# Opening joined with the first attention; gathered stages that take y's sums first

## The reference

```python
x = x + layernorm(linear_attention(layernorm(x)))    # elu(.)+1 features, 16 heads
x = x + layernorm(mixture0(layernorm(x)))            # 8 experts, 2 per row, plus a shared one
x = x + layernorm(softmax_attention(layernorm(x)))   # 16 query heads, 4 key heads
x = x + layernorm(mixture1(layernorm(x)))            # 8 experts, 2 per row, plus a shared one
# layernorm(v) = (v - mean(v)) / sqrt(var(v) + 1e-5)
```

## Time and profile before

| | us |
|---|---|
| median of 3 runs | 1946.88 (1940.11 to 1947.62) |
| the profiled execution, whole | 1943.56 |
| its span, first to last instruction | 1941.8 |
| PE busy | 1629.4 (84%) |
| DVE busy | 1432.8 (74%) |
| ACT busy | 1092.0 (56%) |
| POOL busy | 422.2 (22%) |

### The profile page before, as it was taken

One profiled execution on the slowest core, in us unless ns is written; L12 is line 12 of the kernel. 1 busy time (PEld: TensorE's weight loads), 2 busy tenths in 40 slices (PEclk: granted clock), 3 DMA queues, 4 the chain that ended last, 5 costly groups with the idle time before them and its releaser, 6 DMA issues. The chain is left out here.

```text
span 1941.8 us, 42092 instructions
## 1 busy us (share of the span) xinstructions
PE 1629.4 (84%) x15122; PEld 935.5 (48%) x15122; DVE 1432.8 (74%) x2776; ACT 1092.0 (56%) x2216; POOL 422.2 (22%) x545
## 2 busy tenths in 40 slices
PE   3987469989999993667999999999997857999950
PEld 2775359966666661221222222222223647977730
DVE  5776877744444446869999999999981887756657
ACT  1444635533333333524999999999996454544422
POOL 3000236611221222220000000000000125834432
PEclk9997779999999996876999999999998968999975
DMA  6700025521111114421121121121003303444445
GB/s 248 286 1 6 1 91 168 170 63 61 59 58 60 60 37 147 121 89 50 39 62 44 40 62 41 44 60 40 19 18 110 106 1 100 143 127 124 130 135 168
DMA packets 113091, 164.47 MB, mean 85 GB/s; under 512 B 20278, under 2 KB 89788, under 8 KB 110588
## 3 DMA queue, kind: packets, MB, share of 16 engines
q1 hardware_dynamic: 97372, 117.85, 20.3%
q0 software_dynamic: 15520, 43.93, 6.0%
HBM read 89.07 MB, written 72.37 MB: 83 GB/s over the span
## 5 line engine op out<-in xcount | busy, mean ns | idle before, releaser
L1511 DVE TENSOR_REDUCE sa_row_max<-psum 128x1 f32<-128x1024 f32 x512 | 582.4, 1214 | 12.1 <-PE psum L1393 12.0
L1494 ACT ACTIVATE sa_probs<-psum 128x512 f32<-128x512 f32 x1024 | 549.8, 597 | 37.5 <-PE psum L1444 28.0
L1393 PE MATMUL psum<-v_k_max,v_q_stack 48*128 48x512 f16 x1024 | 301.3, 399 | 24.1 <-DVE sa_row_max L1511 16.2
L1424 PE MATMUL psum<-sa_probs,sa_v_now 128*32 128x256 f32 (+1 forms) x3840 | 321.2, 406 | 0.1
L1444 PE MATMUL psum<-v_q_stack,sa_k_main 49*128 49x512 f16 x1024 | 309.9, 385 | 1.7 <-ACT sa_probs L1494 1.4
L1988 PE MATMUL psum<-m0w_all,m0fx_xt_high 128*128 x568 | 192.7, 381 | 0.5 <-DVE m0fx_xt_low L1920 0.5
L1444 PEld LDWEIGHTS psum<-v_q_stack,sa_k_main 49*128 49x128 f16 x1024 | 64.8, 94 | 221.1 <-ACT sa_probs L1494 209.4
L1424 PEld LDWEIGHTS psum<-sa_probs,sa_v_now 128*32 128x32 f32 x3840 | 75.8, 108 | 190.0 <-issue 100.2
L1934 DVE TENSOR_TENSOR m0fx_ht_low<-psum,m0fx_ht_high 128x512 f16<-128x512 f32 x71 | 49.1, 692 | 134.4 <-ACT m0fx_ht_high L1902 134.4
L1317 POOL TENSOR_SCALAR sa_max_half<-sa_o_sb 128x128 f16<-128x128 f32 x32 | 9.2, 288 | 553.2 <-ACT sa_o_sb L1485 553.2
L1896 ACT ACTIVATE m0fx_gate<-psum 128x512 f32<-128x512 f32 x71 | 42.4, 597 | 152.3 <-PE psum L1988 152.3
(11 more groups left out here) (355 smaller groups left out, 3366.6 us busy)
## 6 DMA issues: line engine op xcount, KB each, us to landing
x_rows<-la_blank SPq DMA_DIRECT2D x18, 1032.0 KB, 8.8
v_q_stack<-q_scratch SPq DMA_DIRECT2D x192, 64.0 KB, 2.4
m0s_all<-x_rows SPq DMA_DIRECT2D x71, 129.0 KB, 2.0
m1fx_x_in<-x_rows SPq DMA_DIRECT2D x71, 129.0 KB, 2.1
m0fs_stage<-in_up SPq DMA_DIRECT2D x16, 512.0 KB, 4.1
m0g_got<-y_rows SPq DMA_DIRECT2D x32, 256.0 KB, 3.8
o_scratch<-sa_o_sb POOLq DMA_DIRECT2D x32, 256.0 KB, 2.5
wo_o_in<-o_scratch SPq DMA_DIRECT2D x32, 256.0 KB, 3.7
```

Source lines behind the costliest of these rows:

```text
L1393: nc.tensor.matmul(mx_ps[m % 2][:, half * 512:(half + 1) * 512], q_stack[h][side:side + ROWS, head, qt * P:(qt + 1) * P], k_max[side:side ...
L1424: last = nc.tensor.matmul(o_ps[32 * g:32 * g + 32, cols], v_now[:, kt, kv, :], probs[(GROUPS * step + g) % 16][:, cols], start=(kt == 0), ...
L1494: nc.scalar.activation(probs[at % 16][:, :], st_ps[bank_of(at)][:, :], ACT.Exp, scale=0.25 / (QK_SCALE * QK_SCALE)).then_inc(s["expd"], 1)
L1511: nc.vector.tensor_reduce(row_max[n % 2][:, at % QT, column:column + 1], mx_ps[m % 2][:, :], AX.X, ALU.max).then_inc(s["maxed"], 1)
```

## The change

It does two things.

1. `x_statistics` goes away as a block of its own. Its instructions move into `linear_attention`. x is loaded in five pieces: tiles 0 to 3, tiles 4 to 7, and the three other batches. DVE counts and sums only the first piece, takes the remainders of the weights and then normalises; the second piece is counted after the third normalisation. The other batches are counted in the slots of the batch before, two tiles at the end of each of slots 0 to 3 and the sums at the end of slot 3. POOL's powers of the first two pieces stand before the masks and the blank tiles, the other three among the numberings 3, 6 and 9 of the blanks. SP issues the x loads before the blank stores.
2. In the gathered stages DVE takes y's counts and sums right after the rows are added, and the adds to x, with x's counts and sums, later in the step; the low parts of x come last. POOL makes y's power before x's. ACT scales before it normalises, and keeps the three high parts before it raises x's.

```diff
-                    x_statistics(core, x_dram, a["qkv0"], qkv_high, qkv_low)
# linear_attention
+    PIECES = ((0, G), (G, TB)) + tuple((b * TB, (b + 1) * TB) for b in range(1, B))
+    COUNTED_IN = TB // 2
# SP
+                load_x(0)
+                for k in range(KD):
+                    sp.dma_start(given[:, k, :], w_dram[k * P:(k + 1) * P, :]).then_inc(w_in[k], 16)
+                load_x(1)
                 sp.dma_start(bias_q[:, :], bias_q_col).then_inc(s["bias_in"], 16)
                 sp.dma_start(bias_kv[:, :], bias_kv_row.to_broadcast([P, 2 * D])).then_inc(s["bias_in"], 16)
+                for n in range(2, len(PIECES)):
+                    load_x(n)
# POOL
+                for n in range(2):
+                    powers(n)
...
                 for q in range(CHUNKS):
+                    if q % 3 == 2:
+                        powers(2 + q // 3)
# DVE, norm(i, j)
+                    for n, (first, last) in enumerate(PIECES):
+                        if i == first:
+                            dve.wait_ge(stats.mean_done, n + 1)
+                            dve.wait_ge(rstd_done, n + 1)
# DVE, end of slot(b, w)
+                    if b + 1 < B and w < COUNTED_IN:
+                        if w == 0:
+                            dve.wait_ge(x_in[b + 2], 16)
+                        for u in range(2):
+                            count((b + 1) * TB + 2 * w + u)
+                        if w == COUNTED_IN - 1:
+                            aggregate(b + 2)
# DVE, ahead of the slots
+                dve.wait_ge(x_in[0], 16)
+                for i in range(G):
+                    count(i)
+                aggregate(0)
+                for k in range(KD):
+                    lower_weights(k)
                 norm(0, 0)
                 norm(1, 1)
                 low(0, 0)
                 norm(2, 0)
+                dve.wait_ge(x_in[1], 16)
+                for i in range(G, TB):
+                    count(i)
+                aggregate(1)
                 low(1, 1)
# gathered_residual, POOL
-                for g in range(NG + 2):
-                    if qkv is not None and g >= 2:
-                        x_norm.power(pool, g - 2, (g - 2) * G, (g - 1) * G, core.minus_half)
-                    if 1 <= g <= NG:
-                        y_norm.power(pool, g - 1, (g - 1) * G, g * G, core.minus_half)
+                for g in range(NG + 1):
+                    if g < NG:
+                        y_norm.power(pool, g, g * G, (g + 1) * G, core.minus_half)
+                    if qkv is not None and g >= 1:
+                        x_norm.power(pool, g - 1, (g - 1) * G, g * G, core.minus_half)
# ACT
+                    if 1 <= g <= NG:
+                        scale(g - 1)
                     if qkv is not None and 2 <= g < NG + 2:
                         normalise(g - 2)
-                    if 1 <= g <= NG:
-                        scale(g - 1)
-                    if following:
-                        keep_high(g - 3, 0)
+                    if qkv is not None and g >= 3:
+                        for m in range(3):
+                            keep_high(g - 3, m)
                     if qkv is not None and 2 <= g < NG + 2:
                         for p in pairs_of(g - 2):
                             raise_high(p)
-                    if following:
-                        keep_high(g - 3, 1)
-                        keep_high(g - 3, 2)
```

More of the change, by code:

```diff
@@ L784, in slot @@
                         parts_q(g, 1)
+                for k in range(KD):
+                    act.wait_ge(w_in[k], 16)
+                    nc.scalar.activation(qkv_high[:, k, :], given[:, k, :], ACT.Copy).then_inc(w_high_done, 1)
                 high(0, 0)
                 high(1, 1)
+                act.wait_ge(s["bias_in"], 32)
                 slots(slot)
@@ L1212, in _ @@
                 for g in range(NG + DRAIN):
-                    if g == 1 and qkv is not None:
-                        weights.vector_low(dve)
-                        bias.vector_rows(dve, core.ident)
                     if g < NG:
@@ L1220, in _ @@
                             add_second(p)
+                        dve.wait_ge(added, 2 * g + 2)
+                        for i in tiles_of(g):
+                            y_norm.count(i, core.y)
+                        y_norm.sums(dve, g, g * G, (g + 1) * G)
+                    if g == 1 and qkv is not None:
+                        weights.vector_low(dve)
+                        bias.vector_rows(dve, core.ident)
                     if 1 <= g <= NG:
@@ L1223, in _ @@
                             add(p)
-                    if g < NG:
-                        dve.wait_ge(added, 2 * g + 2)
-                        for i in tiles_of(g):
-                            y_norm.count(i, core.y)
-                    if qkv is not None and 2 <= g < NG + 2:
-                        for p in pairs_of(g - 2):
-                            lower(p)
                     if qkv is not None and 1 <= g <= NG:
@@ L1234, in _ @@
                             x_norm.count(i, core.x)
+                        x_norm.sums(dve, g - 1, (g - 1) * G, g * G)
                     if qkv is not None and g >= 3:
@@ L1238, in _ @@
                         keep_v(g - 3)
-                    if qkv is not None and 1 <= g <= NG:
-                        x_norm.sums(dve, g - 1, (g - 1) * G, g * G)
-                    if g < NG:
-                        y_norm.sums(dve, g, g * G, (g + 1) * G)
+                    if qkv is not None and 2 <= g < NG + 2:
+                        for p in pairs_of(g - 2):
+                            lower(p)
 def softmax_attention(core, inputs, v_all, o_dram, coming):
```

83 lines of the change are left out of this document (34 added, 49 removed).

## The result

| | median, us | ratio to the kernel before (95% interval) |
|---|---|---|
| before | 1944.74 (1940.11 to 1947.62) | |
| after | 1914.88 (1911.79 to 1918.57) | 0.9849 (0.982 to 0.9879) |
| after, timed again beside a later experiment | 1916.28 (1912.91 to 1918.87), before 1941.71 | 0.9866 (0.9845 to 0.9886) |

A forecast was written before the change was run, and what follows sets the result against it. DVE and what it waits for were taken to set the middle stage, a chain without TensorE the opening. Terms -15.5, -5.0 and -7.6 sum to -28.1 from 1943.56, giving 1915.5, taken as 1916; range 1908 to 1926.

The forecast's parts named there:

- Opening, -20.3: Up to the first attention: half-megabyte load lands at 6.0, first normalisation at 10.9 instead of 29.78; -20.3 us (-17.8 to -21.0).
- Counts and sums in the slots, +3.6: First attention, slots 0 to 3 of batches 0 to 2: 0.6 exposed in batch 0, 1.5 in each of two others; +3.6 us.
- rival (a): First attention: all of DVE's new work is exposed, +8.9 us, giving 1925; chance 0.15.
- Memsets, +1.2: First attention: POOL's blank-tile memsets beside the slots slow normalisations that meet them; 0 to 2.8 us, +1.2 taken.
- First stage in all: Opening and first attention together: -20.3 + 3.6 + 1.2 = -15.5 us.
- Middle gathered stage, -5.0: Middle gathered stage: wait of 1.38 us goes, steps fall from 12.92 to 11.5; -5.0 us, or -2 if projection stays slow.
- The ceiling of 5.6 by the first loads: Middle gathered stage: store queued behind SP's next-attention loads holds up ACT, so the stage gains at most about 5.6 us.
- Last gathered stage, -7.6: Last gathered stage: two waits go, steps fall from 6.91 to 6.01, adds move behind last sums; -7.6 us (-1.3 to -8.5).
- Rival (b): Last gathered stage becomes bound by its transfers, steps stay at 6.91, only 1.3 us gained; +6.3, giving 1922; chance 0.12.
- (c): Opening: the join does nothing, first normalisation still ends up behind POOL or SP; 1931 to 1934; chance 0.05.
- (d): Softmax attention: TensorE's granted clock falls from 0.96; at 0.90 the run is slower, ending at 1954; chance 0.02.

The follow-up runs named there:

- a later experiment: Changed kernel with memsets ahead of the first powers, batches 2 and 3's last counts and sums in the fifth slot, softmax loads in four parts: 1910.24 us, ratio 0.9834.
- join: Kernel before with only the opening joined with the first attention, gathered stages as they were: 1930.43 us, ratio 0.9946.

## Why the prediction was right, and where it was not

- **Opening, -20.3: right** (-20.4), in part by luck: load at 5.94, first normalisation at 10.71, and the second four counts hidden, all as forecast. But the power ended at 10.20, earlier than the sum had it, since its second operation took 1.03 us for 4 tiles where 1.65 for 8 was taken from the earlier trace rows. And the weights, which were put at no cost, came later: their second remainder, behind a wait of 0.81 us, is what the first normalisation followed. The two misses cancel.
- **Counts and sums in the slots, +3.6: right as far as it went.** Without the lower clock it is 0.6 in the first batch (the lead falls from 17.77 to 17.18 us) and 1.5 to 1.7 in each of the two others, so 3.8. The rows behind this term were not those of the slots it speaks of: 85.96 is the second batch's eighth map of k, and the wait at 77.04 lies behind its fifth. The fourth reads the same (71.94 and 72.41, above), and in the kernel before the first three slots of that batch have waits of their own, 1.23, 0.85 and 0.68 us, which catch up their counts. So rival (a), all exposed, is out. What the working did not have is that a pause made on TensorE can be followed by the lower clock: in the profiled execution this doubled the term, +3.2 more. The prediction spoke of the clock only for the gathered and the softmax stages.
- **Memsets, +1.2: too small.** The one normalisation that met them lost 2.6 us, and the pause that this made on TensorE brought 0.6 to 1.0 more in all traces with the hold but the first of after. The value was taken from a row in which two normalisations lost 1.3 us together; how much is lost is set by how much of the memsets is still to come when the normalisation starts. That row shows it too: the two end at 31.90, one normalisation behind the end of the memsets at 31.44. The rule of the Trainium skill ("SBUF — State Buffer", Who interferes with whom), which the prediction weighed and took as the upper end, is that of such an instruction of VectorE and one of GpSimd the one that comes second stands still until the first has ended. The trace agrees: the instruction of 3.00 us stood until the memset beside it was over, and through the second memset as well. The same section of the Trainium skill says that an instruction of VectorE with at most one input in SBUF, outside the modes that use both ports, does not contend with GpSimd. That agrees too: the low part at 18.47, whose other operand is in PSUM, took its usual 0.42 us.
- **First stage in all: -15.5 forecast, -10.4 measured** (last y, 159.77 to 149.41). This is the sum that failed: memsets, put at 1.2 us where the hold cost 2.6, and the lower clock, put at nothing where it cost 3.2, are 4.6 of its 5.1 us. The other 0.4 lies behind the last map of k, in the stretch that scatters.
- **Middle gathered stage, -5.0: too small** (-7.0; 5.5 to 9.8 over all pairs of old and new order). Steps of 11.60 against 11.5 forecast, with VectorE the bound. The ceiling of 5.6 by the first loads came out for the low part that it was worked out for, the seventh group's: counted from the stage's start it ended 5.7 us earlier (838.02 - 738.00 before, 822.63 - 728.28 after), although the loads were issued 6.3 us earlier and not 5.7 (790.37 - 728.28 against 806.43 - 738.00). The step that failed is taking this ceiling for the whole stage. The last two low parts are 10.1 us apart (821.36 and 831.44) where they were 11.4 (836.73 and 848.11). This 1.3 us is TensorE's clock: from the first to the last of the 18 projections between them it is 5.90 us in after and 7.18 before, because fewer of them are slow. It changes from trace to trace with the new order, as said above; both traces with the old order, before and join, have the long form, and whether the order is the reason is not shown.
- **Last gathered stage, -7.6: right** (52.5 to 45.0). Steps of 5.94, no wait. Rival (b), bound by transfers, is out: the rate rose to 278 GB/s with VectorE busy throughout.
- **Rivals (c) and (d)**: the join works alone (10.5 us), and the softmax attention's clock stayed at 0.96.

The sum held because the 5.1 us missing in the first stage and the 2.0 us more in the middle one partly cancel; the profiled execution is also the longest of the four runs of after (1918.57 us), so the median lies nearer to the forecast than the trace does. That it came within 1.2 us is luck: the medians were 29.9 us apart the first time and 25.4 the second.

## What to carry to other kernels

Work moved onto a busy engine is priced by what stands right behind it: two counts were free in three slots, and cost their whole length ahead of the one instruction that TensorE waits for (0.64 and 0.79 us for 0.74 of counts). When such a wait is put on TensorE, look at the spacing of its next matmuls too, since the lower clock can double the price. A long memset on GpSimd belongs where VectorE has nothing to do: here that saved a hold of 2.6 us.

## What was not expected of the hardware

- A pause of 1.90 us on TensorE, in the midst of dense work, was followed by the lower clock (0.51 granted, matmuls of 512 columns 0.43 instead of 0.23 us apart) five times in twelve, and the same program gave different answers at one of its two places. Filled with matmuls that nobody reads, the same place ran at full speed, also with the map of k as late as ever.
- One normalisation, started 0.73 us after two memsets that follow one another (3.57 us together), was held through both and not only through the one that was running: 18.81 to 21.81 us, with the memsets ending at 21.65.
- The middle gathered stage, whose TensorE works in bursts, scatters by 3.6 us (108.2 to 111.8) between traces of the same instructions. The steps that VectorE bounds repeat within 0.02 us, while the last step, bound by TensorE's projection, takes 8.5, 10.1 or 11.45 us as none, some or most of its matmuls run at the lower clock. An edit there is to be judged by its own step and not by the stage's length.
